# First batch prepared by token halves, initial loads reordered, integer weights split in four pieces

## What is computed

```python
paths = jax.nn.sigmoid(x @ Wp + bp)                    # 8 heads x 5
agree = pq * pk + (1.0 - pq) * (1.0 - pk)
sim = jnp.cumprod(agree, axis=-1).sum(axis=-1) / DEPTH # causal mask, softmax over keys
ctx = softmax(sim) @ (x @ Wv)                          # per head, then @ Wo
x = _layernorm(x + ctx @ Wo)
h = silu(x @ wg.T) * (x @ wu.T)                        # int32 weights times 1/127
x = _layernorm(x + h @ wd.T)
```

## Time and profile before

| | us |
|---|---|
| median of 3 runs | 954.82 (953.11 to 960.5) |
| profiled execution | 955.83 |
| its span in the trace | 954.1 |
| PE busy | 848.8 (89%) |
| DVE busy | 478.6 (50%) |
| ACT busy | 455.7 (48%) |
| POOL busy | 227.4 (24%) |

### The profile page before, as it was taken

How to read it: one execution, slowest core, us unless ns; L and a number is a source line. 1 busy time by engine, 2 the same in 40 slices (tenths; PEclk the granted TensorE clock), 3 DMA queues, 4 the chain that set the end, 5 groups by cost and what they waited for, 6 DMA issues and landing times.

```text
span 954.1 us, 15450 instructions
## 1 busy us (share of the span) xinstructions
PE 848.8 (89%) x6146; PEld 412.9 (43%) x6146; DVE 478.6 (50%) x1020; ACT 455.7 (48%) x721; POOL 227.4 (24%) x265
## 2 busy tenths in 40 slices
PE   4389998899989999899988999899988998999764
PEld 3144354443644446344544436344453434444332
DVE  2844346535455426645465355555275353545343
ACT  2255644555445554546445453555546453555211
POOL 0011131223212132122312232132321223231312
PEclk9599999999999999999999999999999999999968
DMA  6831443140511433113431406104321214100000
GB/s 211 213 97 45 89 89 111 45 90 23 141 59 45 111 66 107 72 43 70 89 111 45 89 23 152 70 23 111 82 74 45 64 48 109 47 1 23 1 22 24
DMA packets 44346, 71.09 MB, mean 75 GB/s; under 512 B 3568, under 2 KB 21232, under 8 KB 44272
## 3 DMA queue, kind: packets, MB, share of 16 engines
q1 hardware_dynamic: 44272, 70.07, 28.0%
HBM read 53.28 MB, written 16.78 MB: 73 GB/s over the span
## 4 chain that ended last, share of the span: by engine, by line
PE 73%; ACT 9%; DVE 9%; issue 4%; POOL 3%; DMA 2%; SPq 0%; POOLq 0%; ACTq 0%; DVEq 0%
PE ctx_ps L717 14%; PE misc L752 13%; PE den_ps L717 12%; PE slot L695 11%; PE misc L762 9%; PE misc L671 7%; PE misc L729 6%; ACT probs L409 6%; POOL work L364 2%; PE misc L680 2%; DVE work L548 2%; DVE x L531 1%; ACT work L421 1%; DVE ctx_raw L480 1%; DMA query_stack<-phi_dram 1%
## 5 line engine op out<-in xcount | busy, mean ns | idle before, releaser
L409 ACT ACTIVATE probs<-slot 128x1024 f32<-128x1024 f32 (+3 forms) x384 | 290.3, 808 | 376.4 <-PE slot L695 376.2
L695 PE MATMUL slot<-query_stack,key_stack 128*128 128x512 f16 (+3 forms) x768 | 161.7, 333 | 16.5 <-DMA query_stack<-phi_dram 15.1
L717 PE MATMUL ctx_ps<-probs,vz_sb 128*32 128x512 f32 (+3 forms) x1536 | 166.3, 505 | 10.3 <-DVE ctx_raw L480 8.3
L364 POOL TENSOR_TENSOR work<-work 128x512 f16<-128x512 f32 x96 | 112.7, 1174 | 216.0 <-ACT work L427 215.9
L717 PE MATMUL den_ps<-probs,ones 128*32 128x512 f32 (+3 forms) x1536 | 162.8, 495 | 0.0
L355 POOL TENSOR_SCALAR_AFFINE_SELECT probs<-probs 128x512 f32<-128x512 f32 x128 | 81.8, 641 | 303.9 <-ACT probs L409 302.9
L548 DVE SCALAR_TENSOR_TENSOR work<-work,misc 128x512 f32<-128x512 f32 x96 | 65.8, 686 | 172.7 <-ACT work L421 172.7
L752 PE MATMUL misc<-x1T_hi,w_parts 128*128 128x512 f16 x384 | 147.0, 383 | 5.2 <-DVE x1T_lo L538 2.4
L752 PE MATMUL misc<-x1T_lo,w_parts 128*128 128x512 f16 x384 | 146.5, 382 | 0.0
L695 PEld LDWEIGHTS slot<-query_stack,key_stack 128*128 128x128 f16 x768 | 56.8, 98 | 170.4 <-issue 120.9
L762 PE MATMUL misc<-w_parts,work 128*128 128x256 bf16 x768 | 89.1, 273 | 10.6 <-POOL work L364 10.6
(11 more groups left out here) (52 smaller groups left out, 609.8 us busy)
## 6 DMA issues: line engine op xcount, KB each, us to landing
key_stack<-phi_dram SPq DMA_DIRECT2D x64, 256.0 KB, 5.8
query_stack<-phi_dram SPq DMA_DIRECT2D x64, 256.0 KB, 6.5
xT_sb<-in_xT_dram SPq DMA_DIRECT2D x8, 1024.0 KB, 5.1
x_sb<-in_x_dram SPq DMA_DIRECT2D x8, 1024.0 KB, 5.5
out_dram<-x SPq DMA_DIRECT2D x16, 512.0 KB, 2.9
phi_dram<-phi_hi SPq DMA_DIRECT2D x16, 256.0 KB, 2.0
phi_dram<-phi_lo SPq DMA_DIRECT2D x16, 256.0 KB, 2.3
work<-in_wgT_dram SPq DMA_DIRECT2D x1, 768.0 KB, 8.2
```

Source lines behind the costliest of these rows:

```text
L364: pool.tensor_tensor(hid_lo[:, n % M1, :], hid[:, n % HSLOTS, :], hid_hi[:, n % M1, :], ALU.subtract).then_inc(hid_lo_ready, 1)
L409: act.activation(probs[:, s % P_SLOTS, 2 * p:2 * p + 2, off:CH], slot[p][:, :, off:CH], ACT.Exp).then_inc(slot_drained[p], 1)
L695: mm = pe.matmul(slot[p][:, k, off:CH], key_stack[:, h, P * j:P * (j + 1)], query_stack[:, h, CH * c + off:CH * (c + 1)], start=True, stop ...
L717: mm = pe.matmul(sums[32 * k:32 * k + 32, off:CH], w, probs[:, s % P_SLOTS, k, off:CH], start=first, stop=final)
```

## The change

The first batch is prepared in two halves of 512 tokens. Paths get their own matmuls (`paths`): four tiles of a half side by side in one PSUM tile, 40 columns each; DVE adds the bias straight from PSUM. The value projections of batch 0 then have 256 columns instead of 296 and come behind the features, the last four at the very end; `weigh` waits for them tile by tile. Turns, phi stores and stacks of batch 0 go by group and half, so a stack DMA moves 128 KB, and the first scores of each chunk wait for their own half (four semaphores). The order of the first loads is Wp, the first half of xT, bp, Wv, the second half of xT. The integer weights, Wo and x (`load_rest`) are issued after the first half's stack of group 1. `load_xT(1)` remains the last entry of `first_projections`, behind four half stacks now. The splitting of the integer weights is no longer one piece in step 0: the three matrices are split in steps 0, 6 and 10, the all-reduce goes with the third, the scales come in step 14.

```diff
+    SPLIT_AT = (0, 6, 10, 14)
...
-        plan = [("scale",)]
-        for h in range(2):
-            plan += vz(0, *range(HT * h, HT * (h + 1))) + [("bias", 0, h), ("squash", 0, h), ("features", 0, h)]
-        for c in range(NC):
-            for g in range(NG):
-                plan += turn_f(0, g, c)
-        plan += [("phi_store", 0, 0), ("stack", 0, 0), ("phi_store", 0, 1), ("load_xT", 1)]
-        return plan
+
+        def paths(c):
+            return [("paths", 0, c), ("bias", 0, c), ("squash", 0, c), ("features", 0, c)]
+
+        return ([("scale",)] + paths(0) + vz(0, 0, 1) + turn_f(0, 0, 0) + [("phi_store", 0, 0, 0), ("stack", 0, 0, 0)]
+                + turn_f(0, 1, 0) + paths(1) + vz(0, 2, 3) + [("phi_store", 0, 1, 0), ("stack", 0, 1, 0)]
+                + turn_f(0, 0, 1) + turn_f(0, 1, 1) + vz(0, 4, 5, 6, 7)
+                + [("phi_store", 0, 0, 1), ("phi_store", 0, 1, 1), ("stack", 0, 0, 1), ("stack", 0, 1, 1), ("load_xT", 1)])
...
-            if s == 0:
-                plan += [("weights",)]
+            if s in SPLIT_AT:
+                plan += [("weights", SPLIT_AT.index(s))]
...
-                    sp.dma_start(phi_dram[r, g * P:(g + 1) * P, :], part[:, g, :]).then_inc(phi_stored[g], 16)
+                    sp.dma_start(phi_dram[r, g * P:(g + 1) * P, cols], part[:, g, cols]).then_inc(done, 16)
...
-                        sp.dma_start(dest[32 * q:32 * q + 32, 4 * g:4 * g + 4, :],
-                                     phi_dram[r, g * P:(g + 1) * P, :].rearrange("(h p) n -> p h n", p=NF))\
-                            .then_inc(stacks_in[g], 16)
+                        sp.dma_start(dest[32 * q:32 * q + 32, 4 * g:4 * g + 4, cols],
+                                     phi_dram[r, g * P:(g + 1) * P, cols].rearrange("(h p) n -> p h n", p=NF))\
+                            .then_inc(done, 16)
...
+            sp.dma_start(wvp_sb[:, :, D:VZ], Wp.rearrange("(k p) n -> p k n", p=P)).then_inc(wp_in, 16)
+            sp.dma_start(xT_sb[:, :, 0:CH], xT_v[0, :, :, 0:CH]).then_inc(first_xT_in[0], 16)
+            sp.dma_start(bp_sb[:, :], bp.rearrange("(a n) -> a n", a=1).partition_broadcast(P)).then_inc(bp_in, 16)
+            sp.dma_start(wvp_sb[:, :, 0:D], Wv.rearrange("(k p) n -> p k n", p=P)).then_inc(wv_in, 16)
+            sp.dma_start(xT_sb[:, :, CH:T], xT_v[0, :, :, CH:T]).then_inc(first_xT_in[1], 16)
+            def load_rest():
+                for n, w in enumerate((wgT, wuT)):
+                    sp.dma_start(w_int[n].rearrange("p (k n) -> p k n", k=KD),
+                                 w.rearrange("(k p) n -> p k n", p=P)).then_inc(ints_in, 16)
+                sp.dma_start(w_int[2].rearrange("p (m n) -> p m n", m=M1),
+                             wdT.rearrange("(m p) n -> p m n", p=P)).then_inc(ints_in, 16)
+                sp.dma_start(wo_sb[:, :, :], Wo.rearrange("(k p) n -> p k n", p=P)).then_inc(wo_in, 16)
+                sp.dma_start(x_sb[:, :, :], x_v[0, :, :, :]).then_inc(x_in, 16)
...
                 elif what == "stack":
                     stack(*n)
+                    if n == [0, 1, 0]:
+                        load_rest()
...
-                elif what == "weights":
+                elif what == "weights" and n[0] == 2:
                     pool.wait_ge(w_max_ready, 4)
                     pool.partition_all_reduce(w_gmax[:, :], w_max[:, :], P, RMAX).then_inc(w_gmax_ready, 1)
...
+                if b == 0:
+                    k, n = MISC["paths", 0, h]
+                    if h == 0:
+                        dve.wait_ge(bp_in, 16)
+                    dve.wait_ge(misc_filled[k], n + 1)
+                    dve.tensor_tensor(z_sb[:, HT * h:HT * (h + 1), :],
+                                      misc[k][:, 0:HT * HD].rearrange("p (t n) -> p t n", n=HD),
+                                      bp_sb[:, :].rearrange("p (a n) -> p a n", a=1).to_broadcast([P, HT, HD]),
+                                      ALU.add).then_inc(misc_drained[k], 1)
+                    dve.wait_ge(misc_drained[k], n + 1)
+                    dve.sem_inc(z_ready, 1)
+                    return
...
+            def paths(b, h):
+                k = claim("paths", b, h)
+                if h == 0:
+                    pe.wait_ge(wp_in, 16)
+                pe.wait_ge(first_xT_in[h], 16)
+                for t in range(HT):
+                    for d in range(KD):
+                        mm = pe.matmul(misc[k][:, HD * t:HD * (t + 1)],
+                                       xT_sb[:, d, (HT * h + t) * P:(HT * h + t + 1) * P], wvp_sb[:, d, D:VZ],
+                                       start=(d == 0), stop=(d == KD - 1))
+                mm.then_inc(misc_filled[k], 1)
...
+                if j == 0 and b == 0:
+                    pe.wait_ge(first_stacks_in[g][c], 16 * STACK_DMAS)
+                elif j == 0 and c == 0:
+                    pe.wait_ge(stacks_in[g], 16 * STACK_DMAS * b)
...
-                if i == 0:
+                if b == 0 and g == 0 and j >= TC * c:
+                    k, n = MISC["vz", 0, j]
+                    pe.wait_ge(misc_drained[k], n + 1)
+                elif i == 0:
                     pe.wait_ge(u_ready, 2 * (b + 1))
```

More of the change, by code:

```diff
@@ L111, in between @@
             n[at] += b
-            if 0 <= n[at] < B and (what not in ("load_x", "load_xT") or n[at] > 0):
+            if 0 <= n[at] < B and (what not in ("load_x", "load_xT", "stack") or n[at] > 0):
                 found += [(what, *n)]
@@ L149, in seq_postln_kernel @@
     for what, *n in PLAN:
-        if what in ("scale", "vz", "turn_f", "project", "turn_x1", "gate", "up", "down"):
+        if what in ("scale", "paths", "vz", "turn_f", "project", "turn_x1", "gate", "up", "down"):
             k = len(MISC) % 2
@@ L153, in seq_postln_kernel @@
             misc_uses[k] += 1
+    TURNS = {tuple(n): at for at, n in enumerate([n for what, *n in PLAN if what == "turn_f"])}
     NORM = {tuple(n): at for at, n in enumerate([n for what, *n in PLAN if what == "stats"])}
@@ L226, in seq_postln_kernel @@
         x_in = sem("x_in")
-        weights_in = sem("weights_in")
+        wp_in = sem("wp_in")
+        wv_in = sem("wv_in")
+        bp_in = sem("bp_in")
+        first_xT_in = [sem(f"first_xT{c}_in") for c in range(NC)]
+        first_phi_stored = [[sem(f"first_phi{g}{c}_stored") for c in range(NC)] for g in range(NG)]
+        first_stacks_in = [[sem(f"first_stacks{g}{c}_in") for c in range(NC)] for g in range(NG)]
         ints_in = sem("ints_in")
@@ L287, in load_x, with phi_store @@
                 sp.dma_start(x_sb[:, :, :], x_v[b, :, :, :]).then_inc(x_in, 16)
-            def phi_store(b, g):
-                for c in range(NC):
-                    k, n = MISC["turn_f", b, g, c]
+            def phi_store(b, g, c=None):
+                for half in range(NC) if c is None else (c,):
+                    k, n = MISC["turn_f", b, g, half]
                     sp.wait_ge(misc_drained[k], n + 1)
-                if b >= 1:
-                    sp.wait_ge(stacks_in[g], 16 * STACK_DMAS * b)
+                if b == 1:
+                    for half in range(NC):
+                        sp.wait_ge(first_stacks_in[g][half], 16 * STACK_DMAS)
+                elif b >= 2:
+                    sp.wait_ge(stacks_in[g], 16 * STACK_DMAS * (b - 1))
+                cols = slice(0, T) if c is None else slice(CH * c, CH * (c + 1))
+                done = phi_stored[g] if c is None else first_phi_stored[g][c]
@@ L382, in vz_out @@
                 act.wait_ge(misc_filled[k], n + 1)
-                act.activation(vz_sb[:, b % 2, t, :], misc[k][:, 0:VZ], ACT.Copy).then_inc(misc_drained[k], 1)
+                cols = D if b == 0 else VZ
+                act.activation(vz_sb[:, b % 2, t, 0:cols], misc[k][:, 0:cols], ACT.Copy).then_inc(misc_drained[k], 1)
             def squash(b, h):
@@ L396, in phi_high @@
                 if b >= 1 and c == 0:
-                    act.wait_ge(phi_stored[g], 16 * 2 * b)
+                    if b == 1:
+                        for half in range(NC):
+                            act.wait_ge(first_phi_stored[g][half], 16 * 2)
+                    else:
+                        act.wait_ge(phi_stored[g], 16 * 2 * (b - 1))
                 act.activation(phi_hi[:, g, CH * c:CH * (c + 1)], misc[k][:, :], ACT.Copy,
@@ L632, in _ @@
                 elif what == "weights":
-                    split_weights()
+                    if n[0] < 3:
+                        split_weight(*n)
+                    else:
+                        ffn_scales()
                 elif what == "normalise":
@@ L668, in project_in @@
                 if t == 0:
[L669 removed]
+                    if b == 0:
+                        pe.wait_ge(wv_in, 16)
+                    else:
+                        pe.wait_ge(xT_in, 16 * b)
+                cols = D if b == 0 else VZ
                 for d in range(KD):
[L671 removed]
+                    mm = pe.matmul(misc[k][:, 0:cols], xT_sb[:, d, t * P:(t + 1) * P], wvp_sb[:, d, 0:cols],
```

(2 more changed lines are left out.)

56 lines of the change are left out of this document (24 added, 32 removed).

## The result

The changed kernel takes 980.96 us in the median, against 953.99 for the kernel before in the same comparison: a ratio of 1.0277 (95% interval 1.0244 to 1.0311), 27 us slower. The shift has to be looked for in the 25.1.

A forecast was written before the change was run, and what follows sets the result against it. PE was taken as the bound, so only its waits before the first gate matmul count. +10.9 + 2.0 - 2.0 + 6.1 + 4.2 = +21.2 us gave 976 against the median of 954.82, range 963 to 988.

The forecast's parts named there:

- xT of batch 1 at 57.0: Step 2: batch 1's xT, last in the load queue, lets its first projection start at 57.0 instead of 46.06, +10.9 us.
- By bytes: Half-row stack transfers were priced by bytes moved at 218 GB/s, not at the full price per row.
- Projections start cold, +2.0: Batch 1's first projections run at half pace after PE has stood still for some 20 us: +2.0 us.
- POOL's stall at step 1 gone, -2.0: Weighing of step 1 no longer waits for a mask behind POOL's all-reduce, now at step 10: -2.0 us.
- Piece 1, +6.1: Step 6: splitting the second integer matrix on DVE delays batch 1's second bias add and features by its whole length, +6.1 us.
- Piece 2 and the call, +4.2: Step 10: the third split and POOL's all-reduce, taken as 6.8 us, delay the reciprocal square root and x1's turn: +4.2 us.
- The clock behind the new stalls: Longer cold stretches of PE after each new stall; no term in the sum, only covered by the range's upper end, 988.
- xT comes in time: Rival: batch 1's xT passes the other loads and lands by 36, giving 953 us, not slower; chance 0.05.
- The pieces are hidden: Rival: DVE and POOL waits occur, but PE had as much to wait for anyway; only +10.9, 966 us; chance 0.12.
- Half rows at full price: Rival: each half stack takes a full one's time, 19.2 us more on xT's way, 995 us; chance 0.08.

The follow-up runs named there:

- e3_piece1_first: The changed kernel with the second integer matrix split in step 0 behind the first one, instead of in step 6: 973.21 us.
- e4_reduce_later: The changed kernel with POOL's all-reduce moved from step 10 to step 12, behind the reciprocal square root and that step's mask: 975.76 us.
- e2_one_step: The changed kernel with all pieces of the integer weights, the all-reduce and the scales back in step 0: 964.17 us.
- e6_best: The changed kernel with integers and Wo loaded behind xT's second half, batch 1's xT behind first-half stacks, x last, matrices split in step 0, all-reduce in step 8: 945.99 us.
- e1_xt_early: The changed kernel with the load of batch 1's xT right behind the first half's stack of group 1, ahead of integers, Wo and x: 958.77 us.
- e5: The kernel before with only the integer weights split in steps 0, 6 and 10, the all-reduce with the third, scales in step 14: 968.90 us.

## Why the prediction was right

The forecast was 976 in a range of 963 to 988; 980.96 was measured. Direction and mechanism were those of the forecast: xT late, the pieces visible. The size came out in part by luck: one step was wrong and hit nearly the right number, and one term was missing. The terms one by one:

- *xT of batch 1 at 57.0; 57.66 (landing at 57.54).* Right, though its parts erred both ways. The paths took 3.61 us, not 5.4, and their second half 1.98; but they began at 6.21, not 5.5. On the way the stacks of group 0 landed at 24.4 (forecast 25.4, and the sum went on from 25.2), those of group 1 at 31.6 (32.1), x as the last of `load_rest` at 43.1 (42.1), the second half's stacks at 55.1 (53.8). SP did not only wait: it stood in its own issues (3.47 us for a single phi store), which no term had; that the ring was full is inferred. The first scores came at 26.8, not 31, which changed nothing, since PE then stood until xT. By bytes was the right choice for the half rows: between 45 and 54 us most slices run near 215 GB/s, as the whole rows did in the earlier trace rows (218), so 1 KB to a row costs half of 2 KB here. The row of GB/s in 40 slices of that window, after:

```profile
GB/s 296 178 228 323 282 323 159 287 246 246 214 282 219 228 219 209 205 214 209 209 209 237 237 219 209 218 209 209 214 205 214 205 260 223 219 219 209 205 214 246
```

- *Projections start cold, +2.0.* The 12 pieces took 5.60 us instead of 2.99: +2.6. The granted clock is 0.50 from 57.66 to 60.00, the lower level. The place from which the term was worked out does not show that: in before the slow first pieces ran with the granted clock listed as 1.00 (9.76 to 14.00). Their half pace has another cause, or one that the list does not show.
- *POOL's stall at step 1 gone, -2.0.* Right; no such wait is in the profile of after.
- *Piece 1, +6.1.* Right: 78.55 to 84.56 in the chain, and 6.1 up to the features in e3_piece1_first.
- *Piece 2 and the call, +4.2.* The wait was 5.18 us, at the place named, and e4_reduce_later shows that it was POOL's. The step itself was wrong. I took the 6.8 us between data and result in the kernel before for the length of the call. What passes there begins when POOL reaches the call; in after it was over long before the data came, and what held the root was the wait behind the call, 6.94. Two errors of nearly equal size cancelled; that the term came out is luck. Of the microsecond that was missing 0.6 is the norm: its four rows took 2.33 us (114.55 to 116.88), not 1.71 as in the earlier trace rows, while POOL ran three masks at the same time. That the two slow each other is only inferred; in e4_reduce_later, with one mask beside them, they took 1.68.
- *The clock behind the new stalls* was left to the range and is the term that was missing. From the turn of x1 to the first gate after took 10.1 us; before, e2_one_step and e6_best, which have no stall there, 8.2. The rows of eight weighing matmuls and of the granted clock:

```profile
103.86 1.06 PE L781 MATMUL ctx_ps<-probs,vz_sb 128*32 128x512 f32 x8
...
118.74 1.91 PE L781 MATMUL ctx_ps<-probs,vz_sb 128*32 128x512 f32 x8
```

```profile
100.00:110.00 10.00, 10.00 (x67) 4.78 (x68) 8.99 (x16) 4.74 (x6) 0.39 (x1) 1.00 0.01 2
110.00:120.00 10.00, 4.82 (x32) 2.32 (x28) 4.11 (x13) 2.93 (x5) 2.95 (x4) 0.85 0.00 0
```

PE stood for 5.2 us, and the eight weighing matmuls behind the turn took 1.91 us for 1.06. Cut finer than in these rows, the granted clock is 0.54 from 116.94 to 118.74 and 0.50 from there to 120.45, the lower level. That stretch cost 1.8 us. At the features after has one too, but there before has it as well, behind its own wait of 1.84 us, so against before it adds nothing; the versions that run there at 1.00 gain 1.5.

In sum: 21.2 forecast, 25.1 in the profiled executions. Of the 3.9 about 0.7 is xT, 0.6 the cold start, 1.2 the stretch up to the turn of x1 and 1.8 the clock behind it; 0.3 comes back after the gate.

Of the rivals, "xT comes in time" was refuted by the 26.42 us of waiting, and e1_xt_early shows what it would have brought: not 953 but 959, because the cold start did not fall away (5.27 us for the first projections, 2.99 before), and the turn of x1 with the clock behind it cost 7.1 where the sum has 4.2. "The pieces are hidden" fell with e2 to e5; only piece 2's own work on DVE was hidden, not the call behind it. Half rows at full price fell with the row of GB/s.

## What to carry to other kernels

When work is brought forward, look at the first thing that the early work will wait for next and find its place in the queue: here a load that nobody had been waiting for became the last of 51 transfers, and moving that one DMA was worth 22 us of the 27 lost. Work that fills an engine's idle time has to move with that idle time; piece 1, put between a producer and the work that PE was already waiting for, cost its whole length, piece 2's DVE work had slack behind it and cost hardly anything, and a stall can cost clock as well: behind the 5.2 us at x1 it was 1.8 us. A wait measured once, between data and result, need not be a duration: ask from which moment it runs before it is moved.

## What the runs showed of the hardware

- A tensor_tensor on POOL behind a partition all-reduce started 7.02 us after it with all data there, the call itself 5.59 us after the mask ahead of it; both run in the shadow of a wait, if POOL is already at the instruction: in after the call followed its data by 0.13 us, in e6_best the first tensor_tensor behind the call followed its data by 0.09.
- 16 weight loads of 128x128 f32 with 40 columns behind each took 1.98 us in the second half and 3.61 in the first, 0.124 and 0.226 each, with the granted clock listed as 1.00 both times, so it does not tell them apart. The single loads are listed with 186 to 333 ns in after, 261 in the mean; all 32 together were busy for 5.3 us, not 8.4, so the durations overlap and must not be added up.
- Behind the issues of the integers and Wo (2.5 MB), the next two DMA issues held SP for 3.11 and 3.47 us instead of 0.43.
